# Second attention of a four-layer sequence: global keys laid out on the diagonal, normalisation in two parts

## The chip, the cores and the metric

The kernel runs on one core of a Trainium2 chip. Its time is the device time of one execution in microseconds (us): lower is better. Three executions of the kernel before took 1106.26, 1109.06 and 1099.58 us; the median is 1106.26 us. A further execution, under the profiler, took 1103.31 us.

## What is computed

Sixteen sequences of 256 tokens with 128 features pass through four layers, each followed by a residual sum and a layer normalisation:

1. causal attention with 16 heads of 8 features and rotary positions;
2. a mixture in which each token goes through one of eight 128x128 experts;
3. the second attention, which this change is about: 16 heads of 8 features, with biases. Each head has two softmaxes. The local one runs over the 65 keys within 32 positions of the query, the global one over 25 keys at given positions:

```
s_loc = einsum('blhd,blwhd->bhlw', Q, Kw) * scale     # window of 65 keys
local = einsum('bhlw,blwhd->blhd', softmax(s_loc), Vw)
s_g   = einsum('blhd,bghd->bhlg', Q, K[:, global_indices]) * scale
glob  = einsum('bhlg,bghd->blhd', softmax(s_g), V[:, global_indices])
out   = (0.7 * local + 0.3 * glob) @ Wo.T + bo
```

4. a mixture that sends each token to two of eight experts (512 hidden features), weighted by a softmax of its two best router scores.

## The kernel before

Everything is one program on one core, layer after layer. The order of the work on each engine is written out by hand; engines wait for each other through semaphores that count finished instructions. An engine runs its own list strictly in order, so a wait holds up all that stands behind it.

**The second attention** is `Attention("l1", True, ...)`. The functions `attention_pe`, `attention_act`, `attention_dve`, `attention_pool` and `attention_sp` each run `body(i, p, th)` for i = -1 to 19. Iteration i works on several sequences at once: it prepares sequence i+1 (projection, split into a high and a low part, transposition), scores sequence i for its maxima ("pass 1"), does the exponentials and the sums of sequence i-1 ("pass 2", `pv`), and finishes sequence i-2 (normalisation, output projection, residual, layer normalisation). So the iterations 1 to 15 hold all of pass 1, pass 2 and `pv`; those from 2 on also a finish, and those from 4 on (the "pairs") the routing of two sequences for layer 4 over every two iterations.

An iteration has four **quarters** j = 0 to 3, one for each group of four heads, and a quarter has four **units** u = 0 to 3. In the notation below, (1,2) is quarter 1, unit 2. Heads lie so that partition group 32j to 32j+31 of the queries holds the features of the heads 4t+j; t = 0 to 3 counts along the free dimension.

- **Pass 1**, `pass1(j, u)` (L342): two products of 128x186 scores (160 window keys and 26 global keys) into one of two banks. VectorE adds the mask and takes the maxima from the bank (L663, L671). The bank of unit u is free again when the maxima of unit u-2 are taken.
- GpSimd splits the maxima into a high and a low part by five operations (L843 to L852), TensorE turns them (`round_mx`, L172), ScalarE copies them (L492), and SyncE sends them by a DMA into four spare rows of the queries of their group (L1005). With these rows, pass 2 subtracts the maximum inside the product.
- **Pass 2**, `pass2(j, u)`: units 0 to 2 score the window keys, transposed (L372). Unit 3 scores the global keys (L366): four products of a 128x32 matrix in full float32, side by side in four column groups of the array. ScalarE takes exponentials (L528), GpSimd zeroes what lies outside the window (`mask_window`, L893).
- **`pv(j, part)`**, one quarter after its pass 2: parts 0 and 1 multiply with the window values (L406, 32-column products side by side), part 2 with the global values (L398): the 128x128 matrix `vgb`, which holds the global values of the four heads on its diagonal blocks, times the 256 columns of exponentials.
- **The finish**: ScalarE copies the local and the global sums out of PSUM (L477, L479), `round_ot` and `round_og` turn them (L168), VectorE's `normalise` (L592 to L604) divides both and adds them, `round_ont` turns the sum, `round_y` projects it (L267). GpSimd adds the bias to the residual input (`add_bias`, L899), VectorE adds (L691) and takes mean and variance; GpSimd raises to the power -1/2 (`inverse_deviation`, L906, L908); VectorE scales (`layernorm`, L705).
- **Preparation**: `round_pj` (L253) projects, `round_stack` turns, `round_kg` (L296) picks the global keys by a product with a 0/1 matrix at (3,3); VectorE's `keep_kg` lays them behind and before the window keys (L624) and, with two constant rows added, into `kg` (L625). `round_vg` (L247) and `keep_vg` (L615) do the same for values.
- **Routing**: `round_rt`, `round_rl` (L311) in even iterations, `round_rp` (counts by products with `tri` and `ones` in full float32, L319, L322) at (0,0) of odd ones; GpSimd's `send` scatters 128 rows at a time by an indirect DMA (L923).

The small `mi` banks 0 and 1 of PSUM are used in rounds in a fixed order (`ROUNDS`, L157): each round waits until what the round before it in its bank wrote has been read. `mx0` follows `og` in bank 0, and `pj1` follows `ot` in bank 1; both wait for `on_done`, the end of the whole `normalise`. The lines of this order:

```
ROUNDS = (("pj0", "og", "mx0", "ont", "mx1", "y", "q1", "xt", "mx3"),
          ("rp", "ot", "pj1", "rt", "q0", "vg", "rl", "mx2", "k0", "k1", "kg"))
```

## Time and profile before

| | us |
|---|---|
| median of three runs | 1106.26 |
| profiled execution | 1103.31 |
| its span | 1101.6 |
| TensorE busy in the span | 953.2 |
| VectorE busy | 781.5 |
| GpSimd busy | 678.9 |
| ScalarE busy | 577.6 |
| second attention: first to last pass 1 | 453.7 to 838.7 |
| mean granted TensorE clock, share of full speed | 0.924 |

The span is the profiler's time from the first instruction to the last. In the profile, PE is TensorE's matmuls, PEld its weight loads, DVE VectorE, ACT ScalarE, POOL GpSimd, SP SyncE. A product in full float32 appears as two instructions, one in the rounded form (fp32r) as one. Ends of matmuls are modelled: a matmul's duration holds the latency of the array, and the distance between the starts of two groups says better what the first of them costs.

### The profile page before, as it was taken

What the parts mean: (1) busy time and instruction counts of PE and PEld (TensorE: products, weight loads), DVE (VectorE), ACT (ScalarE), POOL (GpSimd) and SP (SyncE); (2) the same over time, 40 slices, a digit from 0 to 9 for tenths busy, and PEclk for the clock granted to TensorE, in tenths of its full rate; (3) what the DMA queues carried; (4) which work ended last, traced back from release to release, by engine and by line L of the source; (5) the groups of instructions that cost most, each with busy time, mean ns of one, the idle gap of its engine ahead of it and who ended that gap; (6) DMA issues with size and microseconds to landing.
All of it is one profiled execution on the core that took longest, in us unless ns stands there. A gap on an engine that the chain in (4) does not pass through costs nothing.

```text
span 1101.6 us, 27734 instructions
## 1 busy us (share of the span) xinstructions
PE 953.2 (87%) x7536; PEld 699.0 (63%) x7536; DVE 781.5 (71%) x3615; ACT 577.6 (52%) x1250; POOL 678.9 (62%) x1491
## 2 busy tenths in 40 slices
PE   3999999999959995799999999999999319999940
PEld 1777777777735552677777777777776218777830
DVE  3788888888825776457786877777775327888846
ACT  2566676666621332255555555555545007777734
POOL 3566666666631322266769888887879523777765
PEclk9899999999978998599999999999989559999975
DMA  6121111211042441111112121212211166777717
GB/s 184 27 52 32 45 45 31 48 27 45 23 132 91 161 164 80 32 47 34 47 29 59 39 59 48 68 44 60 53 32 38 44 173 234 238 234 250 254 58 212
DMA packets 71375, 98.34 MB, mean 89 GB/s; under 512 B 13688, under 2 KB 43256, under 8 KB 71104
## 3 DMA queue, kind: packets, MB, share of 16 engines
q1 hardware_dynamic: 61040, 83.31, 25.9%
q0 software_dynamic: 4992, 10.30, 2.8%
q10 hardware_dynamic: 5232, 3.42, 1.2%
q8 instruction: 49, 0.80, 0.3%
q14 instruction: 62, 0.51, 0.1%
HBM read 49.48 MB, written 24.77 MB: 67 GB/s over the span
## 4 chain that ended last, share of the span: by engine, by line
PE 73%; DVE 10%; issue 5%; DMA 3%; POOL 3%; ACT 2%; SPq 2%; DVEq 0%; ACTq 0%; POOLq 0%
PE bank L342 6%; PE bank L172 5%; PE bank L253 5%; PE bank L351 4%; PE bank L372 4%; PE bank L1491 4%; PE bank L1492 4%; PE bank L1257 4%; PE bank L1493 4%; PE bank L406 4%; PE bank L168 3%; PE bank L413 3%; PE bank L346 3%; PE bank L381 3%; PE bank L398 2%
## 5 line engine op out<-in xcount | busy, mean ns | idle before, releaser
L528 ACT ACTIVATE p<-bank 128x480 f32<-128x480 f32 (+1 forms) x448 | 240.5, 540 | 247.8 <-PE bank L372 88.0
L663 DVE CUSTOM_DVE_ANT_0 bank<-bank,band 128x160 f32<-128x160 f32 x512 | 156.9, 347 | 82.0 <-PE bank L342 79.5
L663 DVE CUSTOM_DVE_ANT_0 bank<-bank,causal 128x128 f32<-128x128 f32 (+1 forms) x512 | 169.4, 386 | 56.1 <-PE bank L346 40.3
L893 POOL TENSOR_SCALAR_AFFINE_SELECT p<-p 128x380 f32<-128x380 f32 (+1 forms) x256 | 146.5, 602 | 57.2 <-ACT p L528 56.2
L1669 POOL DMA_INDIRECT y_rows<-p,rows x92 | 105.9, 1151 | 67.5 <-DVE p L1622 46.2
L663 DVE DVE_READ_ACCUMULATOR2_ANT nm<- 128x1 f32 x1024 | 143.6, 140 | 0.1
L874 POOL TENSOR_SCALAR_AFFINE_SELECT p<-p 128x256 f32<-128x256 f32 (+1 forms) x192 | 91.0, 486 | 68.3 <-ACT p L528 64.6
L342 PE MATMUL bank<-ks,qs 128*128 128x186 f32 x512 | 118.6, 316 | 3.5 <-issue 2.3
L342 PEld LDWEIGHTS bank<-ks,qs 128*128 128x128 f32 x512 | 81.5, 198 | 38.2 <-issue 23.3
L372 PE MATMUL bank<-qs,ks 128*128 128x160 f32 x512 | 102.2, 303 | 0.0
L1562 ACT ACTIVATE p<-bank,wb 128x512 f32<-128x512 f32 x92 | 63.6, 691 | 39.5 <-PE bank L1493 37.6
L923 POOL DMA_INDIRECT xr<-xs,placei x64 | 65.1, 1017 | 26.7 <-DVE xs L773 14.8
L372 PEld LDWEIGHTS bank<-qs,ks 128*128 128x128 f32 x512 | 76.1, 195 | 7.8 <-issue 0.6
L172 PE MATMUL bank<-identr,ts 128*128 128x128 f32 x512 | 70.3, 264 | 7.0 <-POOL ts L864 6.3
L1612 DVE TENSOR_TENSOR ks<-p,ts 128x512 fp32r<-128x512 f32 x92 | 64.5, 702 | 13.7 <-ACT ts L1565 12.1
L1257 PE MATMUL bank<-p,expert 128*128 128x512 f32 x128 | 67.1, 607 | 0.7 <-DVE p L1316 0.7
L172 PEld LDWEIGHTS bank<-identr,ts 128*128 128x128 f32 x512 | 54.7, 145 | 19.1 <-issue 11.6
L351 PE MATMUL bank<-ks,qs 128*128 128x256 f32 x256 | 63.0, 330 | 0.3 <-DVE nm L663 0.3
L253 PE MATMUL bank<-w_qkv,xt 128*128 128x384 f32 x128 | 62.0, 572 | 1.3 <-ACT xt L484 1.0
L406 PE MATMUL bank<-p,vb 128*32 128x160 f32 x1024 | 61.6, 312 | 0.9 <-POOL p L893 0.5
L351 PEld LDWEIGHTS bank<-ks,qs 128*128 128x128 f32 x256 | 40.0, 197 | 26.4 <-issue 24.8
L381 PE MATMUL bank<-qs,ks 128*128 128x256 f32 x256 | 56.1, 301 | 0.0
(207 smaller groups left out, 2330.0 us busy)
## 6 DMA issues: line engine op xcount, KB each, us to landing
qs<-parts SPq DMA_DIRECT2D x46, 512.0 KB, 5.2
qs<-qf SPq DMA_DIRECT2D x128, 128.0 KB, 2.4
rows<-xr SPq DMA_DIRECT2D x23, 260.0 KB, 3.7
parts<-ks SPq DMA_DIRECT2D x8, 512.0 KB, 2.8
xs<-x_b SPq DMA_DIRECT2D x16, 256.0 KB, 4.0
p<-in_w SPq DMA_DIRECT2D x12, 256.0 KB, 3.4
xin<-in_x SPq DMA_DIRECT2D x16, 128.0 KB, 2.2
parts<-qf SPq DMA_DIRECT2D x4, 512.0 KB, 2.7
```

What stands on the lines that cost most here:

```text
L172: return pe.transpose(out.bitcast(F32R), in_, T.identr[:])
L253: m = pe.matmul(T.mi[tau][:, 0:3 * D], T.xt[:, tau * P:(tau + 1) * P], W.qkv[:], start=True, stop=True)
L342: m = pe.matmul(bank[:, c * WG:(c + 1) * WG], q[:, t, tau * P:(tau + 1) * P], k[:, t, lo:lo + WG], start=c == 0, stop=True, skip_group_che ...
L351: m = pe.matmul(bank[:, c * S:(c + 1) * S], q[:, t, P:S], k[:, t, NGE:NGE + S], start=c == 0, stop=True, skip_group_check=True)
L372: m = pe.matmul(bank[:, c * WIN:(c + 1) * WIN], k[:, t, NGE + kt * P:NGE + (kt + 1) * P], q[:, t, lo:lo + WIN], start=c == 0, stop=True, s ...
L406: m = pe.matmul(T.ov[32 * t:32 * t + 32, lo:lo + WIN], T.vb[n][:, part, j, t, :], flat[:, item * WIN:(item + 1) * WIN], start=j == 0 and p ...
L528: act.activation(pb[:, :, :].rearrange("p u c -> p (u c)")[:, lo:lo + cols], bank[:, 0:cols], ACT.Exp, scale=SCALE).then_inc(L.exp_done, 1)
L663: return dve.tensor_tensor_reduce(at, at, mask, -1.0, -BIG, ALU.add, ALU.min, nm[:, item:item + 1])
L874: pool.affine_select(out=at, in_=at, compare_op=ALU.is_ge, fill=0.0, base=0, pattern=[[0, heads], [1, P]], channel_multiplier=-1).then_inc ...
L893: pool.affine_select(out=at, in_=at, compare_op=ALU.is_ge, fill=0.0, base=base, pattern=[[0, 4], [sign, hi - lo]], channel_multiplier=-sig ...
L1257: pe.matmul(T.yb[p][:, :], W.expert[:, e * D:(e + 1) * D], T.xm[e % 4], start=e == 0, stop=e == E - 1).then_inc(M.y_done, 1)
L1669: pool.indirect_dma_start(Z.y_dram[:, :], bass.IndirectOffsetOnAxis(ap=rows[:, a, C_GOAL:C_GOAL + 1].bitcast(I32), axis=0), Z.ys[r][:, a * ...
```

## The change

- The global keys of four heads are laid on the diagonal of a 128-column matrix (`lay_out_kg`, a new step of VectorE at (1,2)), in rounded form. Pass 2 scores them in quarters 2 and 3 alone, two products for each, reading the queries of all four groups from `qf`. `qf` becomes a ring of three, and SyncE sends the turned maxima to `qf` too, by a second DMA.
- The exponentials of the global scores become the stationary operand and the values the moving one (`global_values`), so that the global sums come out turned: `round_og`, the copy L479 and `pv` part 2 fall away. `global_values(0)` stands at (3,1), `global_values(1)` at (0,1).
- `normalise` has a part for the local sums at (0,2) and one for the global sums and the addition at (0,3).
- `round_kg` and `keep_kg` move to the end of the iteration; behind `round_kg` stand two products whose result nobody reads (`keep_array_busy`).
- GpSimd adds the bias at the end of quarter 0 instead of in quarter 2, and splits the maxima by three operations.
- Layer normalisation's last step moves from VectorE to ScalarE, with two small operations more on GpSimd.
- The counts of the routing are in rounded form; the routing's steps and `send` move to later quarters.

```diff
-ROUNDS = (("pj0", "og", "mx0", "ont", "mx1", "y", "q1", "xt", "mx3"),
-          ("rp", "ot", "pj1", "rt", "q0", "vg", "rl", "mx2", "k0", "k1", "kg"))
+ROUNDS = (("pj0", "mx0", "ont", "mx1", "y", "q1", "xt", "mx3"),
+          ("ot", "pj1", "rp", "rt", "q0", "vg", "rl", "mx2", "k0", "k1", "kg"))
...
-            "ot": (L.on_done, k - 1), "og": (L.on_done, k - 1), "ont": (L.ot_kept, k - 1), "y": (L.r_done, k - 1),
+            "ot": (L.rden, 4 * (k - 2) + 2) if L.local else (L.on_done, k - 1), "ont": (L.ot_kept, k - 1), "y": (L.r_done, k - 1),
...
+        def global_values(pair):
+            batch, par = (fin, p) if pair else (i - 1, n)
+            pe.wait_ge(L.exp_done, L.unit2(batch + 1, 2 + pair, 3) + 1)
+            if pair == 0:
+                pe.wait_ge(L.vg_kept, batch + 1)
+                wait(pe, L.on_done, batch)
+            for tau in range(2):
+                out = T.og[:, tau * S:(tau + 1) * S].rearrange("p (r t z) -> p r t z", r=2, t=4)
+                for t in (2 * pair, 2 * pair + 1):
+                    m = pe.matmul(out[:, :, t, :], T.pg[pair][:, t % 2 * S + tau * P:t % 2 * S + (tau + 1) * P],
+                                  T.vgb[par][:, t, :].rearrange("p (r z) -> p r z", r=2),
+                                  start=tau == 0 and t == 0, stop=True, skip_group_check=True)
+            if pair:
+                m.then_inc(L.pg_done, 1)
...
+        def keep_array_busy():
+            wait(pe, L.red_done, L.units * (4 * i + 3) + 3)
+            for _ in range(2):
+                pe.matmul(T.s1[0][:, 0:P], T.ident[:], T.ident[:], start=True, stop=True)
...
             if u == 0 and j == 0:
                 pe.wait_ge(L.k_kept, 2 * i + 2)
                 if L.local:
-                    pe.wait_ge(L.kg_kept, i + 1)
+                    pe.wait_ge(L.kg_kept, 2 * i + 1)
+            if L.local and u == 2 and j == 0:
+                pe.wait_ge(L.kg_kept, 2 * i + 2)
...
             if L.local and u == 3:
-                for t in range(4):
-                    m = pe.matmul(bank[32 * t:32 * t + 32, 0:S], T.kg[par][:, t, :], q[:, t, :].bitcast(F32),
-                                  start=True, stop=True)
+                pe.wait_ge(L.kd_done, i)
+                for c in range(2):
+                    t = 2 * (j - 2) + c
+                    m = pe.matmul(bank[:, c * S:(c + 1) * S], T.kg[n][:, t, :], T.qf[(i - 1) % 3][:, t, :],
+                                  start=c == 0, stop=True, skip_group_check=True)
...
-            if part == 2:
...
-                m = pe.matmul(T.og[:, r * S:(r + 1) * S], T.vgb[n][:, j, :], pb[:, 3, 0:S],
-                              start=j == 0, stop=False, skip_group_check=True)
...
-                if j == 0 and u == 0 and in_iteration("rp", i, p, th):
-                    round_rp()
-                if j == 0 and u == 2 and th.finish and L.local:
-                    round_og()
-                if j == 1 and u == 2 and in_iteration("rt", i, p, th):
-                    round_rt()
-                if L.local and (j, u) == (3, 3) and th.prep:
-                    round_kg()
-                if th.late and u > 0:
+                if th.late and u in (1, 2):
                     pv(j, u - 1)
+                if L.local and (j, u) == (3, 1) and th.late:
+                    global_values(0)
+                if L.local and (j, u) == (0, 1) and th.finish:
+                    global_values(1)
+                if (j, u) == (1, 1) and in_iteration("rp", i, p, th):
+                    round_rp()
+                if (j, u) == (1, 1) and in_iteration("rt", i, p, th):
+                    round_rt()
...
+        if L.local and th.prep:
+            round_kg()
+            keep_array_busy()
...  ScalarE
-                act.copy(T.ogs[:, :, :], T.og[:, :].rearrange("p (r q) -> p r q", r=2)).then_inc(L.ov_kept, 1)
+            if L.local and u == 3:
+                wait(act, L.pg_done, i - 1)
+                act.activation(T.pg[j - 2], bank[:, :], ACT.Exp, scale=SCALE).then_inc(L.exp_done, 1)
+                return
+        def layernorm():
+            act.wait_ge(L.rstd, L.deviation_steps * (fin + 1))
+            for tau in range(2):
+                act.activation(W.x_next[:, 2 * fin + tau:2 * fin + tau + 1, :], T.r[:, tau:tau + 1, :], ACT.Identity,
+                               scale=T.rs2[:, tau:tau + 1], bias=T.shift[:, tau:tau + 1]).then_inc(L.x_out, 1)
...  VectorE
+            if part == 0:
+                dve.reciprocal(T.rd[:, 0, :], heads[:, :, DH]).then_inc(L.rden, 1)
+                dve.wait_ge(L.rden, 4 * fin + 1)
+                dve.tensor_tensor(on, heads[:, :, 0:DH],
+                                  T.rd[:, 0, :].rearrange("p (h o) -> p h o", o=1).to_broadcast([P, 32, DH]),
+                                  ALU.mult).then_inc(L.rden, 1)
+                return
+            dve.wait_ge(L.pg_done, fin + 1)
             dve.reciprocal(T.rd[:, 1, :], glob[:, :, DH]).then_inc(L.rden, 1)
...
+        def lay_out_kg():
+            wait(dve, L.p2_done, L.unit2(i - 1, 3, 3) + 1 if i > 1 else 0)
+            own = [P, 4, 4, NG]
+            keys = T.ks[p][:, :, 0:NG].bitcast(F32).rearrange("p t (o g) -> p t o g", o=1).to_broadcast(own)
+            mask = T.diag[:, ::DH].rearrange("p (a j o) -> p a j o", a=1, o=1).to_broadcast(own)
+            dve.tensor_tensor(T.kg[p].rearrange("p t (j g) -> p t j g", j=4)[:, :, :, 0:NG], keys, mask,
+                              ALU.mult).then_inc(L.kd_done, 1)
...
                 if j == 0 and u == L.units - 2 and th.finish:
-                    normalise()
+                    normalise(0)
+                if j == 0 and u == 3 and th.finish:
+                    normalise(1)
+                if j == 1 and u == 2 and L.local and th.scores:
+                    lay_out_kg()
-                if j == 3 and u == 2 and th.finish:
+                if j == 3 and u == 2 and th.finish and not L.local:
                     layernorm()
+        if L.local and th.prep:
+            keep_kg()
...  GpSimd
+                pool.tensor_tensor(nm[:, :, 1, :], nm[:, :, 1, :], nm[:, :, 0, :], ALU.subtract).then_inc(L.msp_hi, 1)
+                pool.tensor_copy(mspr[:, :, 0::2, :], nm).then_inc(L.msp_hi, 1)
+                pool.tensor_tensor(mspr[:, :, 1::2, :], nm, msp[:, :, 0::2, :], ALU.subtract).then_inc(L.msp_done, 1)
...
-            if j == 2 and L.local and th.finish:
-                add_bias()
+            if j == 0 and L.local and th.finish:
+                add_bias()
...  SyncE
+                if L.local:
+                    qf = T.qf[(i - 1 if j == 0 else i) % 3]
+                    sp.dma_start(qf[32 * js + 24:32 * js + 24 + L.parts, :, :].bitcast(F32),
+                                 T.mt[js][0:4 * L.parts, :].bitcast(F32)).then_inc(L.mrow[js], 16)
```

## Rows read from the trace of the kernel before

**Rows 1.** The page: busy time, share of the span and instructions of each engine.

```profile
PE 953.2 (87%) x7536; PEld 699.0 (63%) x7536; DVE 781.5 (71%) x3615; ACT 577.6 (52%) x1250; POOL 678.9 (62%) x1491
```

**Rows 2.** Busy time in two iterations (stretch, us, engines, clock, DMA share, GB/s).

```profile
639.87:664.64 24.77, 24.47 (x238) 18.28 (x237) 18.86 (x114) 13.99 (x34) 21.54 (x54) 1.00 0.23 63
664.64:689.23 24.59, 24.29 (x236) 18.05 (x235) 19.41 (x118) 13.60 (x34) 20.10 (x50) 1.00 0.17 43
```

**Rows 3.** Waits, 500 to 800 us: total us, times, longest us.

```profile
PEld bank L172 <- DVE on L604: 7.8, 13, 0.6
```

**Rows 4.** Timeline, PE, quarter 0 into 1: start, us, engine, line, operation, count.

```profile
546.08 0.47 PE L342 MATMUL bank<-ks,qs 128*128 128x186 f32 x2
546.38 0.60 PE L168 MATMUL bank<-ident,ogs 128*128 128x128 f32 x4
546.74 0.43 PE L372 MATMUL bank<-qs,ks 128*128 128x160 f32 x2
...
547.51 0.47 PE L342 MATMUL bank<-ks,qs 128*128 128x186 f32 x2
...
549.38 0.29 PE L172 MATMUL bank<-identr,msp 128*16 128x128 f32 x2 [0.20 <-DVE on L604]
549.50 0.42 PE L342 MATMUL bank<-ks,qs 128*128 128x186 f32 x2
...
550.96 0.39 PE L168 MATMUL bank<-ident,on 128*128 128x128 f32 x2
```

**Rows 5.** Timeline, PE, the end of quarter 1.

```profile
553.41 0.47 PE L342 MATMUL bank<-ks,qs 128*128 128x186 f32 x2
...
555.33 0.43 PE L342 MATMUL bank<-ks,qs 128*128 128x186 f32 x2
```

**Rows 6.** Timeline, PE, end of an iteration and start of the next.

```profile
565.59 0.47 PE L342 MATMUL bank<-ks,qs 128*128 128x186 f32 x2
565.89 0.98 PE L296 MATMUL bank<-pick,ts 128*128 128x26 f32 x8
566.73 0.28 PE L172 MATMUL bank<-identr,msp 128*16 128x128 f32 x2
...
567.86 0.55 PE L342 MATMUL bank<-ks,qs 128*128 128x186 f32 x2
568.41 0.38 PE L319 MATMUL bank<-both,tri 128*128 128x32 f32 x2
...
569.52 0.89 PE L253 MATMUL bank<-w_qkv,xt 128*128 128x384 f32 x2
```

**Rows 7.** Timeline, DVE, the normalisation and the global keys.

```profile
547.39 0.35 DVE L592 RECIPROCAL rd<-bank 128x32 f32<-128x32 f32 x1
...
548.59 0.73 DVE L604 TENSOR_TENSOR on<-on,ong 128x256 f32<-128x256 f32 x1
...
566.91 0.44 DVE L624 CAST ks<-bank 128x104 fp32r<-128x104 f32 x2
```

**Rows 8.** Busy time in two stretches with TensorE's granted clock behind the engines.

```profile
455.00:460.00 5.00, 4.34 (x14) 2.99 (x12) 3.85 (x26) 0.71 (x2) 0.89 (x6) 0.50 0.00 2
852.00:855.00 3.00, 2.53 (x37) 1.17 (x36) 2.56 (x11) 0.82 (x2) 2.78 (x7) 1.00 0.07 22
```

**Rows 9.** Timeline, all engines, the last finish before layer 4.

```profile
855.86 0.59 ACT L477 COPY ovs<-bank 128x512 f32<-128x512 f32 x1 [2.27 <-PE bank L398]
...
857.59 0.38 PE L319 MATMUL bank<-both,tri 128*128 128x32 f32 x2 [1.76 <-DVE both L743]
...
859.97 1.11 PE L168 MATMUL bank<-ident,ovs 128*128 128x128 f32 x4 [0.48 <-DVE count L752]
...
862.98 0.42 DVE L604 TENSOR_TENSOR on<-on,ong 128x256 f32<-128x256 f32 x1
...
867.82 0.42 DVE L691 TENSOR_TENSOR r<-bank,xb 128x256 f32<-128x256 f32 x1 [3.92 <-POOL xb L899]
...
871.08 1.31 SPq L986 DMA_DIRECT2D xs<-x_b  x2
```

232 lines of the change are left out of this document (117 added, 115 removed).

## The prediction

> **What bounds the kernel now.** The page comes first [rows 1]: TensorE has the most busy time, 87% of the span. That is an average over four layers, so the windows are next: two iterations of the second attention of 24.77 and 24.59 us (24.68 on average) hold 24.47 and 24.29 us of TensorE at the full clock, 21.5 and 20.1 of GpSimd, about 19 of VectorE, 14 of ScalarE [rows 2]. TensorE is the bound, in the order in which its list is written; GpSimd is the next, 3 to 4 us per iteration behind it. The waits name one that TensorE meets in every iteration: the turning of the maxima behind the last step of the normalisation, 0.6 us [rows 3]. So each step is priced in TensorE's list, by the distance from start to start, and other engines count where TensorE waits for them. The change touches only the second attention and the passage behind it.
>
> **Quarter 0 up to `ont`.** Before, 4.88 us pass from pass 1 (0,2) to `ont`: 546.08 to 550.96 [rows 4]. In this stretch `og` (0.36), the global scores, the global sums and the wait fall away, but `ont` still waits for the whole normalisation, which now begins later. On VectorE, counted from pass 1 (0,2): maxima taken at 1.31 (546.08 to 547.39) [rows 4, 7]; the four steps ahead of the addition took 1.20 (547.39 to 548.59), and from the addition's start to TensorE's next step 0.79 (548.59 to 549.38) [rows 4, 7]. Part 0 is two steps, 0.67 with the wait between them: 1.98. Maxima of (0,3), 0.65 (estimated as half of the 1.31, the rest being the way from TensorE): 2.63. Part 1 is two steps with a wait, 0.79, and the addition, 0.79: 4.21. TensorE itself would be at `ont` earlier: `pj1` waits for part 0 alone and starts at about 2.1, and `ont` is 1.2 behind it (part of 549.50 to 550.96) [rows 4], at 3.3. So a wait of 0.9 us stands before `ont` in place of the 0.6 before `mx0`, and the stretch takes 4.21 (taken as 4.23): 0.65 saved. Behind `ont` on TensorE's list are pass 2 and `pv`, and all the rest; nothing passes it.
>
> **Ends of the quarters 1, 2 and 3.** From pass 1 (1,3) to pass 1 (2,0) 1.92 us pass [rows 5]. What stays is pass 1 (0.30, as 546.08 to 546.38), the maxima's turn (0.12, 549.38 to 549.50) and four transpositions (0.36 to 0.40, as `og`) [rows 4]: 0.80. Saved: 1.12. Quarter 2 ends alike, but gets the new global scores: two rounded products of 256 columns. The nearest row has two of 186 columns in 0.30 [rows 4]; bounds 0.27 and 0.41 (scaled by columns), I take 0.33. Saved: 0.79. In quarter 3, 566.73 to 567.86 holds maxima's turn, global scores and sums, 1.13, and the pass 1 behind is drawn out to 0.55 from 0.30 [rows 6]: 1.2 goes and 0.33 comes. `round_kg` costs 0.84 in either place (565.89 to 566.73). But now pass 1 (0,0) waits for VectorE's copy of its keys. Before, VectorE began it 1.02 after `round_kg` did (565.89, 566.91), and two copies took 0.44 [rows 6, 7]: one and the way back 0.35, so 1.37, of which 0.84 is `round_kg` and 0.39 the two unread products (four instructions, as four in `og`'s 0.36): cover gone, 0.14 of wait stays. Saved: 1.2 - 0.33 - 0.36 - 0.14 = 0.38.
>
> **Global sums.** Two groups of four full-float32 products are added, 16 instructions with a 128x128 weight load each and 64 columns. The nearest row is the count of the routing: ten instructions of full float32 with few columns in 1.11 (568.41 to 569.52) [rows 6], 0.11 each. Cost: 1.74. Bounds: 0.09 each (`og`'s four in 0.36) and 0.2 (load and product one behind the other: 0.08 for a load, 18.28 us for 237 of them [rows 2], and 0.09 for the product, rounded up).
>
> **Counts in rounded form.** Ten instructions become five in every second iteration: 0.55 per pair, 0.27 per iteration.
>
> Sum per iteration: 0.65 + 1.12 + 0.79 + 0.38 - 1.74 + 0.27 = **1.47 us**. That is 17.6 for the iterations 4 to 15. The iterations 2 and 3 have no counts (1.2 each, 2.4); iteration 1 has no finish, so neither its wait nor `global_values(1)`: about 2.5. Sum 22.5.
>
> **What lies beside it.** GpSimd's split of the maxima in three steps instead of five and two small steps for the shift nearly cancel; the bias moves from its fullest quarter into quarter 0, and its 20 to 21.5 us stay below 23.2. VectorE gives up the layer normalisation, and ScalarE, which has 10 us free, takes it. If that cover were gone, GpSimd's time is the floor: a period of 21.5, so it can't make the kernel slower. SyncE's second DMA per quarter stands ahead of the next step of its queue, but the rows sent at a quarter's end are read a whole quarter later. `lay_out_kg` is no row: 400 elements from two SBUF inputs. The addition, 256 such elements, took 0.42 while GpSimd was idle and 0.73 while it was busy [rows 7, 9], so 0.5 to 1.2; quarter 1 has that much free on VectorE, and at 1.2 TensorE would wait 0.3 for the maxima of (1,3). I take nothing and keep 0.3. (The Trainium skill, SBUF — State Buffer, "Who interferes with whom": a VectorE instruction with two SBUF inputs and a GpSimd instruction that reads SBUF exclude each other, and the later one waits in full. By it `lay_out_kg` takes the high end, and the period loses these 0.3, 4 us in all; the two durations agree with it.)
>
> **Behind the last iteration.** From the copy at 855.86 to the gather at 871.08 the finish is a chain. `ot` waited for the counts (0.59 of copy would let it start at 856.45; it started at 859.97): 3.5 gone. The residual waited for the bias, which stood behind three sends: of 867.82 about 1.9 gone [rows 9]. New in the chain are `global_values(1)`, 1.8 at the lower clock (the counts' ten instructions took 857.59 to 859.97), and the counts and positions, now ahead of the residual on both lists: 1.0. The last counts are halved: 1.1 gone. Sum 3.7.
>
> Total 26.2. The sum is made against the profiled execution's 1103.3 us, which lies 3 under the median and within the three runs: 1103.3 - 26.2 = **1077 us**.
>
> **Rivals.**
> 1. *The waits don't form.* VectorE ends part 1 before TensorE is there, since the addition meets no GpSimd step (0.31 less) and `global_values(1)` gives VectorE time ahead of (0,2). For it: that product block stands in between. Against: the chain above starts at pass 1 (0,2), behind it. 0.9 + 0.14 in 14 iterations and the low ends of the products, 4: 1077 - 18 = **1059**. Chance 0.14.
> 2. *The gain is handed back.* The 16 weight loads aren't overlapped (0.2 each: 1.4 more per iteration, 21 in all), or the masks of GpSimd, with less time per quarter, come later than `pv` asks. Against: a row of overlapped loads with few columns exists. **1098**, within 1%. Chance 0.20.
> 3. *The clock falls.* TensorE gets two waits per iteration, at (1,1) and at the start. In 455 to 460 it had waits between short groups and was granted 0.50, 1.2 GHz, though it was busy in 4.34 of 5 us; in 852 to 855, busy in 2.53 of 3, it was still granted 1.00, 2.4 GHz [rows 8]. The second row speaks for me: gaps larger than mine did not bring it down. Price: a quarter of 5.8 us at the lower clock costs about 5 more. Five such quarters give all back, eight make the kernel slower by over 1%; one in each of 15 iterations gives 1077 + 75 = **1152**. Chance 0.08. (The Trainium skill, TensorE: Matmul & The Clock Gate, "A second HAM failure mode": short idle times between groups of products can make the clock swing between its levels. By that page it would be this rival and its 1152.)
> 4. *The change does not shorten TensorE's list.* The old groups of 32 columns ran side by side and may overlap more than the starts show, so that pass 2's new groups cost what they replace. Then only the tail and the counts are left: **1095**. Chance 0.06, beside rival 2.
>
> **Numbers.** My forecast has 0.52, with a range of its own of 1067 to 1088 (0.3 for `lay_out_kg`, the bounds of the scores, a wait of 0.6 to 1.4 before `ont`). The range to 1059 and up to 1098 with its run to run spread takes in rivals 1, 2 and 4: 1057 to 1101. A difference of 1%, 11 us, is about what a measurement tells from no change. Faster: the forecast, rival 1, and half of rivals 2 and 4, which end about the bound of 1095: 0.77, less 0.03 kept for what isn't named, 0.74. Same: 0.16. Slower: rival 3 and unnamed cost, 0.10.
>
> **What would show it.** The period in the windows: 23.2 us, with the clock at 1.00. In TensorE's timeline: `ont` released by the addition, after a wait of about 0.9; no wait before `mx0`; eight instructions of `global_values` in about 0.87; two rounded products of 256 columns in about 0.33; pass 1 (0,0) within 0.2 of the unread products. GpSimd busy about 20 us of each period. The gather behind the last layer normalisation some 11 us behind its copy instead of 15. I'm wrong if the period is above 24 or below 22.5, if the clock shows 0.50 behind 480 us, or if `pv` waits for masks.

## The result and the profile after

The changed kernel takes 1089.1 us in the median (1088.4 to 1097.4), 0.987 [0.983, 0.991] of the kernel before. The forecast was 1077 with a range of its own of 1067 to 1088; the gain is 1.3% where 2.4% were forecast, a little over half. Ratios here leave out executions more than 1.5% above the fastest of the same kernel, so a median over all of them can lie above its ratio: below, seven of ten are left out of the ratio with the residual sum first, and four of ten of the one with `ont` later.

The profiled execution: 1088.4 us, span 1086.7 (before 1101.6), granted clock 0.919 (before 0.924). The page, in the columns of [rows 1]:

```profile
PE 927.2 (85%) x7176; PEld 705.4 (65%) x7176; DVE 770.8 (71%) x3535; ACT 579.1 (53%) x1234; POOL 667.5 (61%) x1396
```

26 us of TensorE's work are gone, as forecast in kind, and only 15 us of the span. Two iterations of the second attention, 8 and 9 (stretch, us, engines, clock, DMA share, GB/s), beside [rows 2]:

```profile
628.10:652.07 23.97, 22.85 (x218) 18.82 (x217) 18.52 (x109) 14.08 (x32) 20.57 (x47) 1.00 0.22 60
652.07:676.28 24.21, 22.61 (x211) 18.01 (x210) 18.97 (x111) 13.80 (x32) 20.30 (x46) 1.00 0.20 52
```

The period, the time from one `round_kg` to the next, fell from 24.7 to 24.1 us in these two and to 24.0 in the mean of the iterations 4 to 13, not to 23.2. TensorE is now idle in 1.1 and 1.6 us of it, before in 0.3. The waits name what it stands for (500 to 800 us: total us, times, longest), beside [rows 3]:

```profile
PE bank L183 <- DVE on L648: 6.5, 12, 0.6
...
PEld bank L275 <- DVE on L637: 4.3, 12, 0.4
PEld bank L187 <- ACT mt L520: 4.0, 8, 0.5
...
PEld bank L187 <- DVE r L740: 2.9, 5, 0.6
...
PEld bank L187 <- DVE count L801: 1.8, 5, 0.5
```

The first answers to the wait of before; the second was forecast; the last three are in no part of the forecast. Quarter 0 into 1 of an even iteration on TensorE (start, us, engine, line, operation), beside [rows 4]:

```profile
628.10 0.96 PE L318 MATMUL bank<-pick,ts 128*128 128x26 f32 x8
...
629.52 0.43 PE L372 MATMUL bank<-ks,qs 128*128 128x186 f32 x2
...
632.24 1.10 PE L251 MATMUL bank<-vgb,p 128*128 128x64 f32 x8
633.15 0.45 PE L372 MATMUL bank<-ks,qs 128*128 128x186 f32 x2
...
635.30 0.91 PE L275 MATMUL bank<-w_qkv,xt 128*128 128x384 f32 x2 [0.19 <-DVE on L637]
...
637.30 0.41 PE L183 MATMUL bank<-ident,on 128*128 128x128 f32 x2 [0.55 <-DVE on L648]
```

The reader sees here the forecast's own steps. `round_kg` (628.10) to pass 1 (0,0) at 629.52 is 1.42, forecast 1.37. `global_values` (632.24) to the next pass 1 is 0.91, forecast 0.87. Pass 1 (0,2) at 633.15 to `ont` at 637.30 is 4.15, forecast 4.23, and the wait of 0.55 before `ont` is the one announced, at 0.9. The end of quarter 1, from pass 1 (1,3) to (2,0), takes 0.74 in even iterations (forecast 0.80).

Where the forecast left out something, all engines, unit (3,0) of the same iteration:

```profile
645.60 0.45 PE L398 MATMUL bank<-later 128*128 128x256 f32 x2
...
646.09 0.60 ACT L556 ACTIVATE p<-bank 128x512 f32<-128x512 f32 x1 [0.77 <-PE bank L398]
...
646.58 0.34 ACT L520 CAST mt<-bank 16x256 fp32r<-16x256 f32 x1
...
646.98 0.54 PE L187 MATMUL bank<-identr,ts 128*128 128x128 f32 x4 [0.37 <-ACT mt L520]
```

The new global scores (645.60) start a 0.60 us exponential on ScalarE at 646.09; the copy of the maxima stands behind it, and the key stack on TensorE waits 0.37 us for that copy. And the end of quarter 2 of an odd iteration:

```profile
621.81 0.41 DVE L740 TENSOR_TENSOR r<-bank,xb 128x256 f32<-128x256 f32 x1
...
622.27 0.54 PE L187 MATMUL bank<-identr,ts 128*128 128x128 f32 x4 [0.39 <-DVE r L740]
```

The stack at 622.27 shares a bank with `y`, so it needs the residual sum (621.81), which stands on VectorE behind places and weights of the choices. Before, the sum ended 1.30 us behind the start of pass 1 (2,3), now about 1.5, but the stack's turn on TensorE came only at 1.43, behind the old global scores and sums, and it did not wait:

```profile
733.40 0.42 DVE L691 TENSOR_TENSOR r<-bank,xb 128x256 f32<-128x256 f32 x1 [0.51 <-POOL xb L899]
...
733.95 0.65 PE L172 MATMUL bank<-identr,ts 128*128 128x128 f32 x4
```

The distances from pass 1 to pass 1 sum this up, in us by quarters: even iterations before 6.42, 5.82, 6.41, 6.12 and after 5.15, 5.86, 5.65, 7.32; odd ones before 7.59, 5.42, 5.47, 6.13 and after 5.14, 6.38, 5.53, 6.88. Quarter 0 gives 1.3 to 2.5; quarter 3 of both and quarter 1 of the odd ones take 0.8 to 1.2 back.

Last, iteration 15, from its start in steps of 5 us. After:

```profile
795.70:800.70 5.00, 4.98 (x47) 4.42 (x46) 3.15 (x21) 3.16 (x7) 4.45 (x12) 1.00 0.20 51
800.70:805.70 5.00, 3.61 (x36) 2.52 (x35) 4.54 (x25) 2.23 (x6) 3.75 (x8) 0.98 0.02 7
805.70:810.70 5.00, 5.00 (x28) 4.14 (x28) 3.11 (x19) 0.91 (x3) 3.21 (x7) 0.50 0.04 13
810.70:815.70 5.00, 5.00 (x34) 3.92 (x33) 2.68 (x20) 1.54 (x3) 1.99 (x4) 0.50 0.07 23
```

Before:

```profile
812.30:817.30 5.00, 3.28 (x28) 2.26 (x27) 4.80 (x22) 1.70 (x5) 4.25 (x14) 0.97 0.24 56
817.30:822.30 5.00, 5.00 (x28) 4.37 (x29) 1.83 (x14) 1.24 (x3) 0.73 (x2) 0.50 0.06 17
822.30:827.30 5.00, 5.00 (x42) 3.86 (x41) 4.26 (x21) 1.83 (x5) 3.00 (x9) 0.84 0.00 2
827.30:832.30 5.00, 5.00 (x52) 3.73 (x52) 3.45 (x25) 2.32 (x6) 4.33 (x12) 1.00 0.07 23
```

PEclk is the column behind POOL's. Both kernels fall to 0.50 (1.2 GHz) within the first 10 us of this iteration, which has no next batch to prepare, after a stretch in which TensorE was busy in 3.61 and 3.28 of 5 us. The kernel before is back at 1.00 (2.4 GHz) after some 7 us; the changed one stays at 0.50 for 30 us. The last finish (start, us, engine, line), beside [rows 9]:

```profile
847.55 0.57 ACT L507 COPY ovs<-bank 128x512 f32<-128x512 f32 x1
...
859.54 1.40 SPq L1043 DMA_DIRECT2D xs<-x_b  x2
```

From ScalarE's copy to the gather 12.0 us pass, before 15.2.

**The account**, in us of span: the second attention started 2.8 earlier (two steps far ahead of it, in layers that the change does not touch, were already 1.6 and 2.2 early, so this is not the change's); its iterations gave 13.7 (from the last key product ahead of iteration 0 to that of iteration 14: 361.2 to 347.5; forecast 22.5 with iteration 15); iteration 15 up to the last copy lost 8.2 (43.6 to 51.8); the last finish gave 3.2 (forecast 3.7), the way to the pads' DMA 1.1, layer 4 behind it 2.3, code that is the same (212 to 215 us in all profiles of this study). 2.8 + 13.7 - 8.2 + 3.2 + 1.1 + 2.3 = 14.9.

The 13.7 are not all of the kind that was forecast. The iterations 0 and 1 gave 4.4 of them, 20.02 to 18.78 and 23.20 to 20.08 us, at mean clocks of 0.56 and 0.93 before and 0.67 and 1.00 after; in the changed kernel's second profile iteration 0 took 19.75 us at 0.57, so most of its 1.2 is of the execution. The forecast had 2.5 for iteration 1 and nothing for iteration 0. The iterations 2 to 14 gave 9.3, forecast 18.6.

### The profile page after: what moved, and what is told of

It is laid out like the page before. It is cut to its first block, busy times and chain, and to the rows that moved or that the text cites. A ratio compares the mean times of both kernels' runs of the same rounds, so it can differ in the third digit from the quotient of the medians.

```text
span 1086.7 us, 26843 instructions
## 1 busy us (share of the span) xinstructions
PE 927.2 (85%) x7176; PEld 705.4 (65%) x7176; DVE 770.8 (71%) x3535; ACT 579.1 (53%) x1234; POOL 667.5 (61%) x1396
## 3 DMA queue, kind: packets, MB, share of 16 engines
q10 hardware_dynamic: 5232, 3.42, 1.2%
## 4 chain that ended last, share of the span: by engine, by line
PE 73%; DVE 10%; issue 6%; DMA 3%; ACT 3%; SPq 3%; POOL 1%; DVEq 0%; ACTq 0%; POOLq 0%
PE bank L372 6%; PE bank L187 5%; PE bank L432 4%; PE bank L404 4%; PE bank L381 4%; PE bank L183 4%; PE bank L1554 4%; PE bank L1556 4%; PE bank L1555 4%; PE bank L1320 4%; PE bank L275 3%; PE bank L251 3%; PE bank L439 3%; PE bank L376 3%; PE bank L413 3%
## 5 line engine op out<-in xcount | busy, mean ns | idle before, releaser
L562 ACT ACTIVATE p<-bank 128x512 f32<-128x512 f32 (+2 forms) x384 | 215.6, 566 | 190.9 <-PE bank L404 102.0
L944 POOL TENSOR_SCALAR_AFFINE_SELECT p<-p 128x380 f32<-128x380 f32 (+1 forms) x256 | 149.1, 611 | 59.0 <-ACT p L562 57.1
L1732 POOL DMA_INDIRECT y_rows<-p,later x92 | 100.6, 1093 | 70.3 <-DVE p L1685 48.9
L404 PEld LDWEIGHTS bank<-qs,ks 128*128 128x128 f32 x512 | 78.4, 200 | 7.4
L187 PE MATMUL bank<-identr,ts 128*128 128x128 f32 x512 | 66.2, 255 | 13.6 <-POOL ts L915 6.3
L432 PE MATMUL bank<-p,vb 128*32 128x160 f32 x1024 | 63.9, 323 | 1.7 <-POOL p L944 1.7
L520 ACT CAST mt<-bank 8x256 fp32r<-8x256 f32 (+1 forms) x128 | 44.8, 350 | 23.0 <-PE bank L187 23.0
```

What stands on the lines that cost most here:

```text
L187: return pe.transpose(out.bitcast(F32R), in_, T.identr[:])
L404: m = pe.matmul(bank[:, c * WIN:(c + 1) * WIN], k[:, t, NGE + kt * P:NGE + (kt + 1) * P], q[:, t, lo:lo + WIN], start=c == 0, stop=True, s ...
L432: m = pe.matmul(T.ov[32 * t:32 * t + 32, lo:lo + WIN], T.vb[n][:, part, j, t, :], flat[:, item * WIN:(item + 1) * WIN], start=j == 0 and p ...
L562: act.activation(pb[:, :, :].rearrange("p u c -> p (u c)")[:, lo:lo + cols], bank[:, 0:cols], ACT.Exp, scale=SCALE).then_inc(L.exp_done, 1)
L944: pool.affine_select(out=at, in_=at, compare_op=ALU.is_ge, fill=0.0, base=base, pattern=[[0, 4], [sign, hi - lo]], channel_multiplier=-sig ...
L1732: pool.indirect_dma_start(Z.y_dram[:, :], bass.IndirectOffsetOnAxis(ap=rows[:, a, C_GOAL:C_GOAL + 1].bitcast(I32), axis=0), Z.ys[r][:, a * ...
```

## The experiments

All are edits of the changed kernel; the last ones build on each other, as told. "Tail" is the time from the key products of iteration 14 to the pads' DMA, the first transfer of layer 4: before 74.8 us, changed 78.8. Distances are those from pass 1 to pass 1.

**The changed kernel again.**

> The changed kernel once more, unaltered. Its spread is in question: kernels that differ from it by one moved step had iterations of 26 to 29 us, at a granted clock of 0.50 to 0.77 there. If the changed kernel is near that edge itself, some of its executions lie 5 to 20 us above 1089 us; if not, all lie within 1086 to 1092.

1090.8 us (1088.0 to 1097.2), ratio 0.985 [0.982, 0.988]. Its profile has the same periods from iteration 1 on to 0.05 us and the same 0.50 from the third 5 us of iteration 15 on (tail 78.4). So the fall in iteration 15 is the kernel's, not the execution's. No other iteration from 1 on fell in these two profiles; this one's span of 1095.5 us comes mostly from the layers ahead, for its second attention begins at 456.2 us and not at 448.2.

**Is a term of the sum mis-sized?**

```
-                    m = pe.matmul(out[:, :, t, :], T.pg[pair]...
+                    for _ in range(2):
+                      m = pe.matmul(out[:, :, t, :], T.pg[pair]...
```

> The changed kernel with each of the 16 small products for the global values issued twice (numerators and denominators double together). The forecast priced 16 of them at 0.11 us each, 1.74 us an iteration. Theory (this term was sized rightly and TensorE is the bound at both places): the period grows by 1.6 to 1.8 us, 16 batches add 26 us: 1115 us. Rival (TensorE waits there anyway, for VectorE at unit (0,1) and for the maxima at (3,1), so that half or more hides): the period grows by 0.9 or less, 1103 us or less. If the granted clock falls at other places the time says little and the period of undisturbed iterations decides.

TensorE, start, us, line:

```profile
650.79 2.00 PE L252 MATMUL bank<-vgb,p 128*128 128x64 f32 x16
652.60 0.44 PE L373 MATMUL bank<-ks,qs 128*128 128x186 f32 x2
```

1124.9 us, ratio 1.017 [1.010, 1.024]. The block of 8 instructions starts 0.91 ahead of the next pass 1, that of 16 starts 1.81 ahead; the period grew from 23.96 to 25.75, by 1.79 for 16 more instructions, 0.112 each. The largest cost of the forecast (1.74) was right, and nothing of it hides. The time lies 10 us above the 1115 that were expected: this profile's second attention begins at 454.2 us and not at 448.2, and its tail is 83.6 and not 78.8.

**The wait before `ont`.** First the transposes alone, one unit later:

```
-                if j == 1 and u == (1 if L.local else 0) and th.finish:
+                if j == 1 and u == (2 if L.local else 0) and th.finish:
                     round_ont()
```

> The changed kernel with the transposes of the normalised values issued one unit later, at (1,2) (ScalarE's copy of them one exponential later as well). TensorE now stands 0.5 to 0.9 us at (1,1) for the last VectorE sum of the normalisation. The theory (that wait is of the in-order queue alone): the distance (1,1) to (1,2) falls from 2.44 to about 1.7, (1,2) to (1,3) grows by the 0.25 us of the transposes, and 0.5 us an iteration, 7 us in all, is saved: 1082 us. Rival (VectorE is the bound over this stretch and the wait returns one unit later, at a bank of the scores): the period stays at 24.0 us and the time at 1089.

TensorE around (1,2):

```profile
641.15 0.66 PE L183 MATMUL bank<-ident,xs 128*128 128x128 f32 x4 [0.90 <-DVE vtmp L696]
...
641.85 0.38 PE L183 MATMUL bank<-ident,on 128*128 128x128 f32 x2
```

1098.9 us (1086.1 to 1112.4), ratio 0.991 [0.986, 0.996], period 24.16 in undisturbed even iterations; two others took 26.8 and 29.3 us at a mean clock of 0.89 and 0.81, the latter behind a wait of 0.90 for the same `vtmp`. The wait did not go: the next group on TensorE's list, the turn of the routed rows (641.15), now waits 0.90 us for `vtmp`, the bias of `pj1` on VectorE, which stands behind the whole normalisation. Then the cause itself, part 1 of the normalisation, behind that bias:

```
-                if j == 0 and u == 3 and th.finish:
-                    normalise(1)
+                if L.local and j == 1 and u == 0 and th.finish:
+                    normalise(1)
```

with the transposes at (1,2) as above.

> The changed kernel with the second part of the normalisation one unit later on VectorE, at (1,0) behind the projections' bias, and the transposes that read it at (1,2). With the transposes alone moved, the distance (1,1) to (1,2) stayed at 2.6 us: TensorE waited there for VectorE's maxima instead. Theory (VectorE's queue from (0,2) to (1,1) is the bound of this stretch, 5.2 us of work in 5 of time): moving 1.3 us of it later shortens (1,0) to (1,2) by 0.5 to 1.0 us and lengthens (1,2) to (2,0) by 0 to 0.5; period 23.5 us, 1083 to 1086 us. Rival (only the place of the wait changes, for VectorE's total over quarters 0 and 1 is the same): 24.0 us and 1089.

TensorE at the same place:

```profile
643.91 0.66 PE L183 MATMUL bank<-ident,xs 128*128 128x128 f32 x4
...
644.93 0.41 PE L183 MATMUL bank<-ident,on 128*128 128x128 f32 x2 [0.17 <-DVE on L648]
```

1083.1 us (1080.3 to 1085.7), ratio 0.979 [0.973, 0.985]. (1,1) to (1,2) fell from 2.44 to 1.47, (1,2) to (1,3) rose from 1.00 to 1.54, `ont` waits 0.17. Even iterations take 23.67 (23.96), odd ones 23.42 (23.95). It was VectorE's order, and not its total.

**The maxima behind the exponential.**

```
+                early = L.local and u == 3 and j > 1 and th.max_step(j)
+                if early:
+                    keep_mx(j)
                 if th.pass2_unit(L.local, j, u):
                     exp(j, u)
```

> The changed kernel with ScalarE's copy of the maxima of quarters 2 and 3 issued ahead of the 128x512 exponential of the global scores of the same quarter, not behind it. The theory: in even iterations the first key stack, at unit (3,0), waits 0.37 us for the copy, which stands behind the exponential of 0.60; taken first, it ends the wait, the distance (3,0) to (3,1) falls from 1.85 to about 1.42, and 9 iterations with 0.4 each save 3.5 us, 1085 to 1086 us. Rival: the exponential is 0.3 us later and what waits for it (global values at (3,1), the next unit's bank) takes the gain back: distance (3,0)+(3,1) stays at 3.8, time 1089.

1090.3 us (ratio 0.986 [0.983, 0.990]). In even iterations (3,0) to (3,1) fell from 1.85 to 1.60, not to 1.42: 23.72 in two and 23.79 in one of them instead of 23.96. Two others took 24.1: `lay_out_kg` took 1.29 us in them instead of 0.69, beside GpSimd's selections, and (2,0) to (2,1) grew from 1.14 to 1.54. Right in mechanism, 60% in size, and too small for the times of whole executions to show.

**The residual sum in odd iterations.** Three orders on VectorE were tried. The weights behind the statistics:

```
-                    if (j, u) == (2, 1):
-                        weights_of_choices()
...
                     residual()
+                if second_half and (j, u) == (2, 2):
+                    weights_of_choices()
```

> The changed kernel with VectorE's three steps for the weights of the choices (odd iterations of the second attention) moved from quarter 2, unit 1, to behind the residual sum of quarter 2, unit 2. The theory (new waits on VectorE's order eat the gain): in odd iterations the query stack at the end of quarter 2 waits for the residual sum, and the distance from the first product of unit (2,3) to that of (3,0) is 1.94 us; the three steps stand ahead of the sum with about 0.5 us, so the distance falls to about 1.5, and 5 to 7 such iterations save 2 to 3 us: 1086 us against 1089. Rival (the products of the change are themselves longer than forecast, the waits only stand beside them): the distance stays near 1.9 and the time at 1089.

An odd iteration, all engines:

```profile
633.45 1.24 DVE L818 TENSOR_SCALAR den<-e 128x4 f32<-128x4 f32 x1
633.53 1.12 POOL L944 TENSOR_SCALAR_AFFINE_SELECT p<-p 128x508 f32<-128x508 f32 x2
...
635.89 0.47 PE L372 MATMUL bank<-ks,qs 128*128 128x186 f32 x2 [0.90 <-DVE nm L720]
```

1119.9 us, ratio 1.016 [1.009, 1.023]: slower than before the change. The distance (2,3) to (3,0) fell to 1.13, as the theory has it. But the weights' first step, 4 elements a partition, took 1.24 us instead of 0.18, beside GpSimd's four selections on `p` (the line shows the last two), and pass 1 behind waited 0.90 for the maxima: (3,0) to (3,1) 2.78 instead of 1.41. The odd period rose to 24.7, and the clock fell (stretch, us, engines, clock):

```profile
680.00:684.00 4.00, 3.42 (x32) 2.58 (x31) 3.90 (x18) 2.07 (x5) 3.73 (x8) 1.00 0.06 21
684.00:690.00 6.00, 5.45 (x43) 4.47 (x44) 2.85 (x21) 2.51 (x6) 4.26 (x9) 0.72 0.44 104
```

Seven iterations took 26.2 to 27.8 us; the 27.8 is an even one, in which another step of VectorE was held up (shown with the fill below). This is the forecast's third rival, in a kernel one step away from the changed one. Then the sum ahead of the weights:

> The changed kernel with the residual sum alone (0.41 us) moved up to unit (2,1) of VectorE in odd iterations, ahead of the weights; the weights stay at (2,1), beside GpSimd's indirect DMA, where their first step takes 0.18 us (moved behind the statistics it fell beside GpSimd's selection on p and took 1.24 us, and the maxima behind it kept TensorE waiting 0.90). Theory: the distance (2,3) to (3,0) falls from 1.94 to 1.1 as there, (3,0) to (3,1) goes to 1.7 at most, since the first key stack then shows its own wait for ScalarE's copy of the maxima, and an odd iteration takes 23.4 us, not 24.0: 5 x 0.5 = 2 to 3 us, 1086 us. Rival (every wait taken away in this half comes back at the next bank): period 23.9 to 24.0, 1089 us or, where the granted clock falls more often, above.

An odd iteration, all engines:

```profile
674.25 0.41 DVE L740 TENSOR_TENSOR r<-bank,xb 128x256 f32<-128x256 f32 x1
...
675.75 0.28 DVE L657 TENSOR_TENSOR vgb<-bank,diag 128x128 f32<-128x128 f32 x1
...
676.08 0.29 PE L187 MATMUL bank<-identr,msp 128*16 128x128 f32 x2 [0.83 <-DVE vgb L657]
```

1112.5 us (1089.5 to 1117.7), ratio 0.990 [0.983, 0.997]: seven of the ten executions lie between 1112 and 1118 us, above the kernel before. The wait did not shrink ((2,3) to (3,0) 2.03): the mask of the global values, pushed behind the weights, now holds the maxima's turn for 0.83 us. Odd iterations 24.4. The profiled execution is one of the short ones; what the long ones did is not shown. Last, sum, mask, weights, on top of the best kernel below:

> The kernel with later normalisation, maxima copied first and the fill in iteration 15 (1076.8 us, odd iterations 23.4), and in odd iterations VectorE's order at unit (2,1) is residual sum, mask of the global values, weights; the statistics stay at (2,2). Theory (the wait of odd iterations at the end of quarter 2 is VectorE's order alone): (2,3) to (3,0) falls from 1.94 to 1.1, (3,0) to (3,1) rises from 1.4 to 1.5, odd iterations take 22.7 us, 5 of them save 3 to 4 us: 1073 us. Rival (given back whatever the order, by the first key stack's wait for the maxima or by VectorE's later maxima): odd 23.3 to 23.5, 1077 us.

Iteration 15, all engines:

```profile
806.11 2.20 POOL L974 TENSOR_SCALAR_AFFINE_SELECT p<-p 128x380 f32<-128x380 f32 x4
...
806.34 2.00 DVE L845 TENSOR_TENSOR xs<-e,xs 128x4 f32<-128x4 f32 x1
...
809.12 0.44 PE L382 MATMUL bank<-ks,qs 128*128 128x186 f32 x2 [1.88 <-DVE nm L739]
```

The stretches of 5 us around it:

```profile
805.50:810.50 5.00, 2.88 (x31) 2.27 (x29) 4.93 (x20) 1.54 (x4) 3.22 (x7) 1.00 0.07 22
810.50:815.50 5.00, 5.00 (x37) 4.15 (x37) 2.05 (x15) 1.19 (x3) 3.19 (x8) 0.59 0.04 13
```

1083.7 us, ratio 0.981 [0.976, 0.986]. Odd iterations took 23.2 instead of 23.4, a fifth of a microsecond and not 0.7: (2,3) to (3,0) is still 1.74. But in iteration 15 the weights' last step took 2.00 us beside a row of selections of 2.20, pass 1 waited 1.88, the clock fell to 0.50 in the next 5 us, and the tail grew from 68.9 to 76.2. Keeping the old order in iteration 15 alone (`moved = second_half and i < B - 1`):

> The kernel before it with the old VectorE order (weights, mask, sum) in iteration 15 and the new one (sum, mask, weights) in odd iterations up to 13. Theory (one long VectorE step in iteration 15 cost the clock of the tail): the tail is 69 to 70 us, the odd iterations keep 23.2, and the time is 1075 to 1076 us. Rival (the clock of the tail is near its edge in any case, chance of the execution): tail 74 to 77 us and 1081 to 1084.

1076.2 us (1071.2 to 1078.0), ratio 0.974 [0.971, 0.977], odd iterations 23.25, tail 68.4. So that one wait was worth 7.8 us of tail. Against the best kernel, 1076.8 us, the moved order itself gives nothing that these times can show.

Where the rest of (2,3) to (3,0) goes, the kernel with sum, mask and weights shows in an odd iteration:

```profile
715.82 0.44 PE L382 MATMUL bank<-ks,qs 128*128 128x186 f32 x2 [0.55 <-DVE nm L739]
```

No stack waits any more; instead pass 1 (3,0) waits 0.55 us for the maxima of (2,2), which VectorE takes behind sum, mask and weights (713.63 to 715.02). Here it is the amount of VectorE's work at this place, and not only its order, as the rival in the expectation has it.

**The clock in iteration 15.** Two unread products of 128x384 in the places of the projections:

```
+                if j in (0, 1) and u == 0 and L.local and i == B - 1:
+                    spare_pj(j)
```

> The changed kernel with two products of 128x384, which nobody reads, in iteration 15, where the projections of a next batch stand in all earlier iterations. In the changed kernel the granted clock falls to 0.50 at about 805 us, behind two waits of 0.5 and 0.9 us in the first quarter of that iteration, and stays there to 835. The theory (the fall costs the tail): with the places filled the clock stays at 1.00 and the stretch from the last global-key product to the last gather falls by 6 to 10 us: 1080 to 1083 us. Rival (the tail is bound by VectorE and the other engines, TensorE's clock changes nothing): 1089 us. Second rival (the fall comes anyway since the waits stay): clock 0.50 from about 805 again.

1093.4 us, ratio 0.991 [0.986, 0.995]. 1.00 until 20 us into the iteration, as the theory has it, then 0.50; tail 77.4. Little or nothing gained: the fall is only put off. Then unread transposes in the places of the stacks as well:

```
+                if j == 3 and u in (0, 2) and L.local and i == B - 1:
+                    spare_stack(f"k{u // 2}")
...
+            if j in (1, 2) and L.local and i == B - 1:
+                spare_stack(f"q{j - 1}")
```

> The changed kernel with unread work in iteration 15 at every place where earlier iterations prepare the next batch: two products of 128x384 and four groups of four 128x128 transposes. With the two products alone the granted clock stayed at 1.00 until about 820 us (805 in the changed kernel) and then fell to 0.50, with nothing gained. The theory (the tail's price is the clock): now 1.00 to about 835, the stretch from the last global-key product to the last gather 4 to 8 us shorter than 63.8 us, time 1083 to 1086. Rival (VectorE, ScalarE and GpSimd set the tail): the same 63 to 65 us and 1089, or longer by the 3 us of unread work.

Iteration 15 from 5 us behind its start (columns as above):

```profile
813.20:818.20 5.00, 4.25 (x40) 3.12 (x39) 4.25 (x23) 1.85 (x6) 3.47 (x9) 1.00 0.02 7
...
823.20:828.20 5.00, 4.50 (x45) 3.36 (x44) 4.90 (x30) 2.42 (x5) 4.24 (x8) 1.00 0.05 18
```

The clock is 1.00 for 25 us and the tail 73.5, 5.3 less than 78.8 in spite of the unread work. The time, 1091.2 us (ratio 0.986), shows none of it: in the profiled execution iteration 12 took 29.4 us, its clock 0.61 and 0.70 in two stretches. What stood ahead of the fall, all engines:

```profile
742.86 2.21 POOL L960 TENSOR_SCALAR_AFFINE_SELECT p<-p 128x380 f32<-128x380 f32 x4
743.14 2.37 DVE L690 TENSOR_TENSOR later<-ks,diag 128x400 fp32r<-128x400 f32 x1
...
746.20 0.51 PE L382 MATMUL bank<-ks,qs 128*128 128x186 f32 x2 [1.31 <-DVE nm L736]
```

`lay_out_kg`, 0.57 to 0.94 us in the other iterations of this profile up to 14, began 0.28 us behind the first of GpSimd's four selections and ended with the last. Pass 1 (2,1) waited 1.31 us for the maxima behind it, and the clock fell 0.3 us later, for 10 us. Up to iteration 14 this is the changed kernel's own list, so it does fall in the middle too, in some executions. The same step took 2.36 us in the even iteration of 27.8 us with the weights late.

**The unread products at each iteration's end**, left out (`keep_array_busy()` not called):

> The changed kernel without the two 128x128 products that nobody reads, which stand at each iteration's end while VectorE adds to the global keys. If they only fill a wait, the distance from the last product group to the next first one stays at 1.4 us and the time at 1089; if they stand on the path, each iteration is 0.2 to 0.3 us shorter, 1085. If they hold the clock (a rival), iterations at 0.50 to 0.80 appear and the time is 1095 or more.

1094.6 us (1086.7 to 1105.0), ratio 0.992 [0.989, 0.995], against 0.985 [0.982, 0.988] for the changed kernel measured beside it. From iteration 1 on every period of its profile is that of the changed kernel to 0.03 us, so the products cost nothing. That they keep executions from falling is suggested by the times; the profiled execution, the shortest of the twelve, does not show such a fall. It shows something else. TensorE's list in iteration 15 is that of the changed kernel, but the clock was at 0.50 for 10 us (it is 1.00 again in 816.80 to 821.80) and not for 30, and the tail is 74.1, 4.6 shorter. So how long this fall lasts is not settled by the waits of iteration 15 alone.

**What works, together.** Later normalisation and the maxima first:

> The second part of the normalisation and its transposes one unit later (which took 0.3 us from odd and 0.5 from other iterations, 1083 us) together with ScalarE's copy of the maxima ahead of the exponential of the global scores (which took 0.25 from even iterations). They act in different halves, so even iterations should take 23.4 and odd 23.4 us: 1081 us. Rival (the second only moves its wait once the first is there): 1083 us.

1082.9 us, ratio 0.979 [0.976, 0.982]; all routing iterations 23.4. The clock is at 0.50 or 0.66 from 15 to 40 us into iteration 15, tail 75.6. With the unread work:

> The kernel before it in this call, with the unread work of iteration 15 at every place of a preparation, which kept the granted clock at 1.00 over the first 25 us of that iteration and shortened the stretch from the last global-key product to the pads' DMA from 78.8 to 73.5 us. Theory: 3 us less than without it, 1078 us. Rival (with fewer waits in the first quarter the clock already comes back after 5 us, as in the kernel with the normalisation later, tail 71.3 us): no less, or 2 us more for the unread work, 1081 to 1083.

Iteration 15 from 10 us behind its start:

```profile
801.80:806.80 5.00, 5.00 (x53) 4.19 (x52) 4.63 (x31) 2.22 (x5) 4.66 (x9) 1.00 0.08 23
...
811.80:816.80 5.00, 3.29 (x34) 2.82 (x34) 1.47 (x10) 3.03 (x7) 4.39 (x11) 1.00 0.06 20
```

1076.8 us (1072.9 to 1078.6), ratio 0.973 [0.970, 0.976], with 0.985 for the changed kernel beside it: it beats the kernel before and the changed one. The clock holds at 1.00 for 25 us, the tail is 68.9, 6.7 less than without, and the forecast 1078 of that text was met. The 6.7 are not the fill's alone as far as these two profiles go: without it `lay_out_kg` of iteration 15 fell beside the selections and took 2.39 us, pass 1 waited 1.42 for the maxima behind it and the clock fell 0.7 us later; with it the step took 0.57. Whether the fill moved that step away or the execution did is not shown.

## Why the prediction was right or wrong

- **Quarter 0 up to `ont`**: right, 4.15 for 4.23, and the two new waits stand where they were put. What the forecast took as the price of the layout was an order that could be mended: 0.3 to 0.5 us an iteration.
- **Ends of the quarters**: the first step that failed. The forecast gave each removed group its full start-to-start distance. For the products themselves that holds: even iterations save 1.17 and 0.91 at the ends of 1 and 2 (forecast 1.12, 0.79). But in odd iterations the end of quarter 2 saves nothing, 1.91 before and 1.94 after, for the removed scores and sums had covered VectorE's late residual sum. The end of quarter 1 saves 0.8, since it now meets the counts, and the end of quarter 3 saves 0.13 where 0.38 was said. (Its terms for quarter 3 give 0.37, not 0.38.) In quarter 3 (3,0) to (3,1) of even iterations grew by 0.44, from 1.41 to 1.85, since the key stack waits for the copy of the maxima: the new exponential was put at nothing on ScalarE, "which has 10 us free". It has them, but not at that place. The forecast's 1.47 is 1.20 for an even and 1.75 for an odd iteration, whose counts it halved; 0.81 and 0.64 were saved. In the iterations 2 to 14 that makes 9.3 missing of 18.6.
- **Global sums**: right, 0.91 a block for 0.87; doubling both blocks cost 1.79 for 1.74.
- **Counts**: right in size, 0.45 and 0.13 between starts for five instructions.
- **What lies beside it**: GpSimd took 20.3 to 20.6 us of each period, as said, and no cover was lost there. `lay_out_kg` took 0.56 to 0.97, between the bounds of 0.5 and 1.2. The upper bound was too low for what can happen: the step took 1.29 us in three iterations of the kernel's neighbours and 2.36 to 2.39 in three, beside GpSimd's selections, and the price was then not 0.3 but up to 1.4 us of wait and a fall of the clock.
- **Behind the last iteration**: its own term held (3.2 for 3.7). The second step that failed is iteration 15 itself, which was summed as one more iteration at the full clock with 1.47 saved: it ran at 1.2 GHz for 30 us instead of 7 and lost 8.2 us. The forecast set rival 3 against every iteration and looked at the clock only in rows around 455 and 852; a row at 812 to 832 of the kernel before would have shown the fall that was already there. That the clock is the cause, and not the waits as such, three pairs of profiles show in part. The fill in the changed kernel adds work and gives 5.3 us of tail; in the best kernels it goes with 6.7, beside a wait that is gone too; and one wait of 1.88 us, far shorter than what it cost, went with 7.8. The other profiles go the same way, though not exactly (one tail of 76.2 stands at 0.73): a mean clock of 0.63 from the key products of iteration 14 to the gather goes with tails of 78.4 to 78.8 (the changed kernel twice, the sum first), 0.72 and 0.73 with 74.1, 73.1 and 71.3 (without the products at the iterations' ends, maxima first, later normalisation), 0.81 and 0.85 with 68.9 and 68.4 (the two best kernels).
- 26.2 were forecast. Missing are 8.8 in the iterations (9.3 in 2 to 14 and the 1.5 of iteration 15, less the 1.9 that 0 and 1 gave beyond the forecast), 8.2 in iteration 15 and 0.5 behind it; 2.8, 1.1 and 2.3 came from outside the forecast's terms: 14.9. Most of these 6.2 is luck, and without them 8.7 would have been left, a third of the forecast: the second attention begins between 447.9 and 456.3 us in the profiles of the changed kernel and its variants, behind layers that are the same in all.
- **The rivals**: 1 and 4 are out, since the waits formed and the list did shorten. 2 had the gain handed back in part (1098), but by mechanisms that did not act: neither the weight loads (0.112 each, not 0.2) nor `pv`'s masks. 3 came true in iteration 15 of this kernel and in the middle of three of its neighbours. The rule cited from the Trainium skill (TensorE: Matmul & The Clock Gate, "A second HAM failure mode") was nearer in kind than the row at 852 that was set against it: here 3.61 us were busy of the 5 ahead of the fall, in many groups. In extent it was not: the iterations 1 to 14 of both profiles kept 1.00, and 1152 was far off.
- Still open: why VectorE's steps meet the selections in some executions and iterations and not in others; what sets the length of the fall in iteration 15; and layer 4's 2 us.

## What to carry to other kernels

When work is taken off the bound engine, walk its list and ask at each removed group which slower step of another engine finished under its cover: that step's end is the new distance, and the gain is only the difference. Check the iterations at the edges of a loop apart: here the last one, with less to do, lost the clock, and the kernel with its gaps filled with unread products was the faster one (1076.8 for 1082.9 us). Look at single iterations and not at their mean: a step of VectorE that is held up once costs a wait, and the wait can cost the clock. And move a cause (the late VectorE step), not the product that waits for it: the wait moves on to the next one in order.

## What the runs showed of the hardware

- A VectorE step of 4 elements a partition took 1.24 us (633.45 in the kernel with the weights late) and 2.00 us (806.34 in the one with sum and mask first), where the same two steps take 0.15 to 0.18 and 0.17 at the least and up to 0.63 and 0.57 in other routing iterations before iteration 15. Each stood beside a row of four GpSimd selections of 0.5 to 0.7 us and ended with the last of them (634.69 and 634.66, 808.34 and 808.31). A tiny step is no tiny step if it falls there; they cost TensorE 0.9 and 1.9 us of wait. (The Trainium skill, SBUF — State Buffer, "Who interferes with whom": of a VectorE and a GpSimd instruction that want the shared pair of ports, the later one waits in full. The 2.00 beside 2.20 agree, but here the step waited through several selections in a row, and the rule speaks of one instruction.)
- The same holds for larger steps. `lay_out_kg` (0.56 to 0.57 us at the least) took 2.37 us beside the four selections in the kernel with the full fill, 2.36 with the weights late, 2.39 in iteration 15 of the best kernel without fill; in the kernel before a scaling step of the layer normalisation took 1.91 (0.34 at the least) in iteration 15. Pass 1 then waited 1.31, 1.31 and 1.42 us for the maxima, and in the kernel before 1.48, up to the copies of its keys (815.30), which stood behind that step and the maxima; the clock fell 0.3 to 2.2 us behind the start of the product that had waited. The hold-up can go the other way: where the step took 1.29, GpSimd's third selection took 0.99 instead of 0.64.
- Granted clock: 0.50 followed on stretches in which TensorE was busy in 3.61 of 5 us (changed kernel), 3.28 of 5 (before), 2.88 of 5 (sum and mask first), and 3.42 of 4 (weights late). The price of one fall was 4 to 5.5 us in the middle (29.4 for 24.0, 27.8 for 24.0), and 5 to 8 us in the tail.
